# Moving an activation-table load by ten slots, and zeroing attention's V tile on another engine

## What is computed

```python
ada = jax.nn.silu(c) @ ada_w + ada_b
shift_msa, scale_msa, gate_msa, shift_mlp, scale_mlp, gate_mlp = jnp.split(ada, 6, axis=1)
x = x + gate_msa[:, None, :] * _attention(_modulate(_layernorm(x), shift_msa, scale_msa), qkv_w, qkv_b, proj_w, proj_b)
x = x + gate_mlp[:, None, :] * _mlp(_modulate(_layernorm(x), shift_mlp, scale_mlp), fc1_w, fc1_b, fc2_w, fc2_b)

# in _attention: n=2 sequences, t=1024 tokens, 16 heads of 18
qkv = (x @ qkv_w + qkv_b).reshape(n, t, 3, H, DH)
attn = softmax(einsum('nthd,ntkd->nthk', q * scale, k))
out = einsum('nthk,ntkd->nthd', attn, v)
```

## Time and profile before

| | |
|---|---|
| median of 3 runs | 421.26 us (420.74, 421.26, 435.42) |
| the profiled execution's own time | 420.82 us |
| its span, first to last instruction | 419.1 us |
| TensorE busy | 395.0 us, 94% |
| VectorE, ScalarE, GpSimd busy | 66%, 55%, 28% |
| mean granted TensorE clock | 0.986 of full speed |

### The profile page before, as it was taken

The page is one execution under the profiler, slowest core; times in us unless marked ns, Lnnn a source line. Parts: engine busy times, 40 slices in busy tenths (PEclk is TensorE's granted clock), DMA queues, the critical chain, the costliest instruction groups (busy, mean ns, idle before and its releaser), DMA issues.

```text
span 419.1 us, 11790 instructions
## 1 busy us (share of the span) xinstructions
PE 395.0 (94%) x4807; PEld 256.2 (61%) x4807; DVE 275.3 (66%) x781; ACT 229.5 (55%) x481; POOL 116.2 (28%) x139
## 2 busy tenths in 40 slices
PE   8999999999989899899979888889999999999996
PEld 4665555666545566667656556568655575666575
DVE  2688885677689856446557256666899776746452
ACT  3356434532267899898877775666775442322200
POOL 6019999973009700000000000006510010101040
PEclk9999999999999999899989899999999999999999
DMA  5999000000000000000000000000000000000011
GB/s 168 300 312 290 21 4 3 1 16 2 2 0 2 2 2 3 3 2 5 2 5 7 3 3 3 2 3 2 2 0 1 16 30 14 29 14 23 21 45 42
DMA packets 7928, 14.72 MB, mean 35 GB/s; under 512 B 2555, under 2 KB 6239, under 8 KB 7748
## 3 DMA queue, kind: packets, MB, share of 16 engines
q1 hardware_dynamic: 7874, 13.96, 11.0%
HBM read 11.52 MB, written 2.38 MB: 33 GB/s over the span
## 4 chain that ended last, share of the span: by engine, by line
PE 65%; DVE 16%; ACT 11%; issue 7%; ACTq 0%; DVEq 0%
PE psum L986 11%; PE psum L528 8%; PE psum L970 8%; PE psum L815 6%; ACT scratch L1081 3%; PE psum L799 3%; PE psum L893 3%; PE psum L628 2%; DVE BN L1319 2%; ACT big L1114 2%; PE psum L640 2%; PE psum L909 2%; DVE scratch L1352 2%; PE psum L584 2%; PE psum L619 2%
## 5 line engine op out<-in xcount | busy, mean ns | idle before, releaser
L970 PE MATMUL psum<-scratch,W 128*128 128x512 f16 (+1 forms) x252 | 57.9, 379 | 0.0
L986 PE MATMUL psum<-W,big 128*128 128x288 f16 x432 | 55.1, 286 | 0.0
L517 POOL TENSOR_TENSOR X<-X,big 128x288 f32<-128x288 f32 x16 | 13.0, 823 | 148.0 <-ACT big L1179 147.6
L1204 ACT ACTIVATE big<-psum 128x512 f32<-128x512 f32 x36 | 21.3, 597 | 57.0 <-PE psum L970 51.9
L815 PE MATMUL psum<-WQ,scratch 128*128 128x288 f16 (+1 forms) x336 | 49.9, 290 | 1.8 <-DVE scratch L1373 0.9
L986 PEld LDWEIGHTS psum<-W,big 128*128 128x128 f16 x432 | 42.2, 98 | 12.9
L528 PE MATMUL psum<-ident 128*32 128x192 f32 (+3 forms) x146 | 44.1, 386 | 0.0
L1142 ACT ACTIVATE big<-psum 128x1024 f32<-128x1024 f32 x32 | 32.8, 1030 | 17.9 <-PE psum L856 17.7
L970 PEld LDWEIGHTS psum<-scratch,W 128*128 128x128 f16 (+1 forms) x252 | 24.7, 98 | 25.6
L815 PEld LDWEIGHTS psum<-WQ,scratch 128*128 128x128 f16 (+1 forms) x336 | 30.2, 99 | 13.3 <-DVE scratch L1373 1.6
L1081 ACT ACTIVATE scratch<-psum,MOD 128x512 f32<-128x512 f32 (+3 forms) x48 | 34.3, 773 | 6.6 <-PE psum L739 4.0
(11 more groups left out here) (221 smaller groups left out, 766.0 us busy)
## 6 DMA issues: line engine op xcount, KB each, us to landing
X<-in_x_dram SPq DMA_DIRECT2D x4, 576.0 KB, 17.9
out_dram<-big SPq DMA_DIRECT2D x16, 144.0 KB, 1.7
big<-in_L_cond_W_dram SPq DMA_DIRECT2D x1, 2268.0 KB
big<-in_L_cond_ada_w_dram SPq DMA_DIRECT2D x2, 864.0 KB, 18.4
stage<-in_L_cond_fc_w_dram SPq DMA_DIRECT2D x1, 1296.0 KB, 18.7
big<-in_L_cond_fc_w_dram SPq DMA_DIRECT2D x1, 1152.0 KB
stage<-in_L_cond_qkv_w_dram SPq DMA_DIRECT2D x1, 864.0 KB
big<-in_L_cond_fc_w_dram SPq DMA_DIRECT2D x3, 144.0 KB
```

What stands on the lines that cost most here:

```text
L970: mm = pe.matmul(FB[idx % 3], W1[0:r, w_, P * m:P * m + P], HT[0:r, n % 2, a_, :], start=(p_ == 0), stop=(p_ == 6))
L986: mm = pe.matmul(YB[t % 2][:, 0:D], g[:, a_, f, cols], W2[:, w_, f, :], start=(f == 0 and a_ + w_ == 0), stop=(f == NF - 1 and w_ == 1))
L1204: act.activation(G32[:, idx % 2, :], FB[idx % 3], ACT.Gelu, scale=1.0 / (FINE * FINE)).then_inc(gelu_sb, 1)
```

## The change

Two edits. `EXP_TABLE_AT` goes from 25 to 35, so that ScalarE's Exp, with the table's load ahead of it, stands at the end of slot 35 instead of slot 25. The two memsets of VG leave VectorE's queue and stand in GpSimd's, ahead of the projection's additions, behind a wait for `tr_ready` = 12 (on VectorE they stood behind a wait for `split_done` = 12, after the 59 slots).

```diff
-        EXP_TABLE_AT = 2 * NQ + 1
+        EXP_TABLE_AT = 3 * NQ - 1
...
             for b in range(B):
                 chain(pool.tensor_scalar(GB2[:, b, :], GATE[:, b, :], FINE * FINE, None, ALU.mult))
                 chain(pool.tensor_tensor(GB2[:, b, :], GB2[:, b, :], B2ALL, ALU.mult))
+            pool.wait_ge(tr_ready, 3 * NCH)
+            pool.memset(scratch[:, 0:4 * CH], 0.0).then_inc(vg_clear, 1)
+            pool.wait_ge(vg_clear, 1)
+            pool.memset(VG.rearrange("p a c g d -> p (a c g) d")[:, :, DH:DH + 1], 1.0).then_inc(vg_clear, 1)
             for t in range(NT):
                 pool.wait_ge(proj_mul, t + 1)
...
-            dve.wait_ge(split_done, 3 * NCH)
-            dve.memset(scratch[:, 0:4 * CH], 0.0).then_inc(vg_clear, 1)
-            dve.wait_ge(vg_clear, 1)
-            dve.memset(VG.rearrange("p a c g d -> p (a c g) d")[:, :, DH:DH + 1], 1.0).then_inc(vg_clear, 1)
-
             def normalise(w):
```

## The result

The changed kernel takes 417.75 us (median of 20 runs, 416.82 to 434.72), the kernel before 421.39 us (median of 20, 419.17 to 435.42). The ratio is 0.9938, with a 95% interval from 0.9918 to 0.9958: 2.6 us less, between 1.8 and 3.5. The forecast was 418.8 us, 2.03 us less. Now and then an execution of either kernel runs at 426 us or more; such runs stand in the medians and ranges, while the ratios leave them out.

A forecast was written before the change was run, and what follows sets the result against it. TensorE was taken to bound the kernel (65% of the chain), with ScalarE setting the pace in slots 26 to 30. The terms -2.28 + 0.25 + 0 + 0 = -2.03 us on 420.82 gave 418.8 us, range 416.6 to 421.0.

The forecast's parts named there:

- The load leaves slot 25: Slots 25 to 30: ScalarE resumes 1.40 us earlier and its 0.88 us wait before slot 28's turn goes, 2.28 us gained.
- The load arrives in slot 35: Slots 35 to 38: ScalarE's delay reaches TensorE's `qkv` of slot 38 as 0.25 us, bounds 0 and 0.96.
- The memsets leave VectorE: End of qkv: VectorE then waits 2.72 us for TensorE anyway, so taking the memsets away is worth 0.
- The memset on GpSimd: Around slot 30: takes about 2 us, at most 5.4, and does not hold VectorE's split; 0 us.
- What would show it: Signs: TensorE gaps under 0.5 us and clock 1.00 in slots 26 to 28, split 0.7 us, attention 2.0 us earlier.
- Rival four: Slot 35: a table switch costs 1.4 us more on ScalarE than in slot 25, giving 420.4 us; chance 0.06.
- One: Slots 26 to 28: the clock falls all the same, the first gain is only 1.40, 419.7 to 420.4 us; chance 0.15.
- Two: Behind qkv: a low-clock stretch goes (417.1 us) or one more comes (420.5 us) with the shift; chance 0.15.
- Three: Slots 30 to 32: GpSimd's memset holds VectorE and the kernel is slower, 422.0 us or more; chance 0.04.
- Five: Whole kernel: the change does nothing because the load is not on the path, 420.8 us; chance 0.03.

The follow-up runs named there:

- experiment three: Kernel before, load still in slot 25, plus seven unread matmuls filling TensorE's 1.79 us wait in slot 27; ratio to the kernel before 0.9985.
- experiment one: Kernel before with only the load moved to slot 35, memsets kept on VectorE; 419.06 us, ratio to the kernel before 0.995.
- Experiment five: Changed kernel with two more table loads in slot 35 (a Sqrt and an Exp behind the first Exp); ratio to the kernel before 1.0015.
- experiment two: Kernel before with only the memsets moved to GpSimd, load kept in slot 25; 420.37 us, ratio to the kernel before 0.9984.
- experiment four: Changed kernel with GpSimd's large memset replaced by a two-input subtraction of the tile from itself; ratio to the kernel before 0.9975.
- Experiment nine: Changed kernel with attention's values matmuls on TensorE ahead of the step's maxima; 418.22 us, ratio to the kernel before 0.9926.

## Why the prediction was right

The sum was -2.03 us; the touched stretches give -2.57 + 0.25 - 0.03 = -2.35 us, and the ratio -2.6 (1.8 to 3.5).

- **The load leaves slot 25**, forecast -2.28, measured -2.57. Of it 1.49 is the load's length (forecast 1.40; slot 26's turn also overlaps the cast ahead of it a little, which it could not do behind a load), and 1.08 is the gap with its low clock (forecast 0.88). The difference of 0.2 in the second lies behind slot 28's turn: from there to slot 32's `qkv` it was 7.63 us and is 7.43. I had counted the wait in front of the turn and not what the low clock cost behind it: before, ScalarE's next cast waits for the `qkv` of 1.72 us and starts 1.46 us behind the start of the turn, now 1.34, and the rest is lost in the handovers after it. In experiment three, where only the clock is mended, the distance is 7.42. Experiment three shows the split, experiment one the sum.
- **The load arrives in slot 35**, forecast +0.25 between 0 and 0.96, measured +0.25 by the chain that was named. Experiment five shows that there was no slack left.
- **The memsets leave VectorE**, forecast 0, measured 0.02 at most (experiment two).
- **The memset on GpSimd**, forecast about 2 us long and no cost: 1.81 us, and a split that overlaps it at its usual length.
- **What would show it**: the gap is 0.29 us, the clock 1.00, the split 0.68. In before's time, which is less 3.21 for this execution, slot 32's `qkv` is at 182.71 (forecast 183.0), the load at 189.19 (189.5), attention's start at 211.39, 2.35 us sooner (2.0). One figure in that list was wrong by its own sum: it said 1.8 us sooner for slot 38's `qkv`, as if the 0.25 had to be taken off twice. -2.28 + 0.25 is -2.03, and 2.32 was measured. Rival four has the same slip: 1.4 us on top of the sum is 420.2 us, not 420.4. And the sentence that ScalarE has no idle time in slots 26 to 30 leaves out the 0.88 us that the paragraph ahead of it counts. No gap of over 0.5 us arose behind slot 36.

The rivals:

- **One** (the clock falls all the same) is refuted: 1.00 over slots 26 to 30, with gaps of 0.29 us and less.
- **Two** (a low stretch behind qkv comes or goes) is half right, and I had it wrongly framed: such a stretch lies behind qkv in all twelve profiles that keep the order of maxima and values, at lengths from 3.4 to 10.2 us, with the change and without. It belongs to the spread of executions rather than to the change. In the two profiles with the values first it is absent. Its price was set too high, at up to 1.7 us for 3.5 us of low clock. In the eight profiles whose load, casts and order leave attention's start alone, the distance from the first to the last exponential is 60.24 to 60.66 us where the stretch lasts 3.4 us, 60.62, 60.70 and 61.15 where it lasts 6.8, and 61.56 where it lasts 10.2. That is about 0.4 us for the second length and 1.1 for the third, a comparison across executions and not an experiment.
- **Three** (GpSimd holds VectorE) is refuted for the memset. The mechanism itself exists: experiment four has it, at +1.37 us. The Trainium skill ("GPSIMD Engine Reference", Key points) says that the two share their SBUF interfaces, and contend when VectorE's instruction has two SBUF inputs. The split has two in both kernels. The trace agrees for GpSimd's subtraction (2.70 us for the split) and not for its memset (0.68), so by these runs it also matters what GpSimd's own operation is.
- **Four** (a switch costs more in slot 35) is refuted: the next cast follows 0.12 us after the load's end there too. The Trainium skill ("ScalarE: Activation LUTs", What ACT_TABLE_LOAD costs) has about 1283 ns for the load, and the traces agree with 1.28 us; its drain of about 1380 ns does not show in either slot, nor in experiment five, where one load follows another after 1.50 us.
- **Five** (no effect) is excluded by the interval.

What stays open: why the low stretch behind qkv is short in one execution and long in another. The order of TensorE's work there seems to bear on it (two profiles against twelve). Experiment nine alone varied only the order, in one profile, and its times are too few to price it.

## What to carry to other kernels

A short one-off operation (a table's load, a priming) belongs where its engine waits for another one anyhow; look for waits ahead of its neighbours rather than for a low busy share, and count how many microseconds of them there are, since the next load costs its full length. Where an engine of the critical chain stands still, price the gap together with the slower matmuls behind it: here 1.49 us of load cost 2.57. When a difference of half a percent matters, compare distances between marks round the edit, not the spans of two executions.

## What the runs showed of the hardware that I had not expected

**The start of the program differs between executions.** The same matmuls, in the changed kernel's first profile and in that of before:

```profile
8.45 1.43 PE L532 MATMUL psum<-ident 128*128 128x320 f32 x2
```

```profile
6.88 0.81 PE L528 MATMUL psum<-ident 128*128 128x320 f32 x2
```

Until about 13.8 us every pair of this shape took 1.38 or 1.43 us in the one, 0.76 or 0.81 in the other, while the granted clock of 4 to 14 us reads 1.00 in both. By 15.7 us the one is 3.24 us behind the other, which makes up the 3.21. The changed kernel's second profile has 0.81 at once. So the record of the granted clock does not tell everything about the matmuls' speed, and no run here says what decides it.

**A two-input operation of GpSimd stops VectorE's two-input operation almost until its own end** (2.70 us instead of 0.68), while a memset of the same 2048 columns, beside which half of the same operation ran, cost it nothing (0.68). The subtraction takes 3.60 us, the memset 1.81.

**A gap of 1.79 us on TensorE cost 1.08 us behind it**, through the matmuls that ran at a granted clock of 0.57; filling the gap showed it. Behind one of 3.06 us 1.51 us were lost at a granted clock of 0.51, which no run tested by filling it.
